# Attention scores in five PSUM banks taken in turn, two banks for the side work, and the second high half on ScalarE

## The chip, the core and the metric

The kernel runs on one core of one Trainium2 chip. The metric is the device time of one execution in microseconds. TensorE is called PE in the profile, VectorE DVE, ScalarE ACT, GpSimd POOL, and SP is the engine that issues most of the DMAs.

## What is computed

The input is x of 2 x 2048 rows with 256 features. A block of three parts is computed: half a feed-forward network, self-attention with 16 heads of 16 features, and half a feed-forward network again.

```
x = x + 0.5 * ffn(layernorm(x))
x = x + attention(layernorm(x))
x = x + 0.5 * ffn(layernorm(x))

ffn(h):  h = s0 * [h, -h] @ sign(k0);  h = 2 * relu(h)      # 256 -> 1024
         h = s1 * h @ sign(k1);        h = 2 * relu(h)      # 1024 -> 1024
         return s2 * h @ sign(k2)                           # 1024 -> 256
attention(h): q, k, v = h @ wq + bq, h @ wk + bk, h @ wv + bv   # per head
         softmax(q @ k.T / 4) @ v, heads side by side, @ wo.T + bo
```

The exponentials dominate ScalarE's work: 2 x 16 x 2048 x 2048 scores, 1,048,576 in each of the 128 partitions.

## The kernel before, in words

Tokens are worked in 8 blocks of 512. A unit u below 8 is the first network on block u, a unit from 8 to 15 is the second on block u - 8. A network has three layers, l1 (8 output tiles m of 128 x 512), l2 (8 tiles) and l3 (2 tiles); around them stand the layer norm (`norm`, `xn`, `split`, `flip`), the projections `qk` (4 tiles) and `v` (2 tiles), the sum of squares `sq` (2 per block, for a guard on the size of the scores) and, ahead of the second network, `heads` and `out`. Activations are kept as two float16 tensors, a high half (`h_hi`) and the rest (`h_lo`): whoever drains a PSUM bank writes first the high half, then `h_lo` as the bank less the high half.

PSUM has 8 banks of 512 float32 columns. Before attention begins, side work goes through seven of them in turn (`WHOLE`), ScalarE writes the high halves and VectorE the low ones.

Attention is 32 groups of 4 heads, 8 steps a group, 256 **steps** in all. The order of a step is written out in the loop `for n in range(att_steps)`; side work of the networks is dealt into it. On PE a step is:

- `score` 0: two pairs of score matmuls (p0, p1). A pair is two matmuls of 64 rows, side by side in the two row halves of the array, into two banks.
- the first part of the side work (S1), a number of matmuls that `PAIRS` gives by kind;
- `score` 1: the third pair (p2);
- the second part of the side work (S2);
- `score` 2: the fourth pair (p3);
- if there is one, a **column** (`sq` or `range`: one small tile in a bank of its own), taken from the list `columns` in steps in which a pair of side tiles has just been finished;
- `values`: 16 records of matmuls that multiply the probabilities of the step before with v, into the accumulating bank `O_BANK` (V).

Side tiles are worked two at a time (`lay_pair`, `pe_pair`): one matmul in the upper row half for the one, one in the lower for its mate, then turned. `PAIRS` deals the slots of a step as 5 and 3 for l2 (10 and 6 matmuls, a pair of tiles in four steps), 10 and 6 for l3, 4 and 4 for l1 (8 and 8 matmuls, a pair of tiles in every step), 1 and 1 for qk (4 and 4 matmuls of float32), 2 and 2 for v and out. Of the 256 steps 144 carry l2, 36 carry l3 and 76 the others. When the tiles of a pair change row halves, PE waits on its own semaphore `halves`; for l1, v and out that falls at the head of S2.

Scores use banks 0 to 3. Pair number e of all writes banks 2 * (e % 2) and the next (`pe_scores`, L737), and waits until exponential e - 2 has been done, since that one read the same banks. ScalarE does nothing in attention but the exponentials (`act_attention`, L808), one of 128 x 1024 for each pair, four a step. Side work, columns among it, goes through banks 5, 6, 7 in turn (`SHARED`); a pair of tiles starts when both of its banks have been drained (`pe_pair`, L683). In attention VectorE drains alone: high half (L857; L873 for qk), low half (L859; L875), high half, low half. The column `sq` is drained by one maximum (L880), behind the pair of its step. At a group's end VectorE copies bank 4 out (L994).

SP reads the same list of steps: it stages q and k of the next group, moves results of a group out, and loads x. None of its steps changes place here.

Of the kernel before, what the change touches and what calls it, by code (L numbers as in the profile page):

```python
# [17 lines left out]
P = 128  # L18
# [5 lines left out]
class Step:  # L24
# [4 lines left out]


    kind: str
    u: int = 0
# [10 lines left out]
    free_act: int = 0  # L43
    free_dve: int = 0
    mate: object = None

# [39 lines left out]
def build(nc, x, wq, bq, wk, bk, wv, bv, wo_t, bo, k0, k1, k2, s0, s1, s2, out):  # L86
# [24 lines left out]
    RING = 4  # L111
    PROB_SLOTS = 8
    GROUP = 4
    groups = batches * qblocks * heads // GROUP
    group_steps = key_tiles // 2
# [4 lines left out]

    WHOLE = [0, 1, 2, 3, 5, 6, 7]
    SHARED = [5, 6, 7]
    O_BANK = 4

# [83 lines left out]
    while not (side[0].kind == "l2" and side[0].u == qblocks + 1):  # L208
        lay(side.pop(0), WHOLE, True)
    scores_free = max(numbers.held[b][0] for b in range(4)), max(numbers.held[b][1] for b in range(4))  # L210

# [31 lines left out]
    def lay_pair(slots):  # L243

        s, t = side[0], side[1]
        if not s.n:
            for bank in (s, t):
                bank.on_act = False
                numbers.lay(bank, SHARED)
                find[bank.kind, bank.u, bank.m] = bank  # L250
            s.hi = 0
        lo, s.hi = s.hi, s.hi + slots
        work.append(replace(s, lo=lo, hi=s.hi, n=2 * s.n, mate=t))
        if s.hi == 2 * s.n:
            s.lo, s.hi = 0, s.n
            work.append(replace(t, lo=t.n, hi=t.n))
            del side[0:2]

    for n in range(att_steps):
        work.append(Step("att", n))  # L260
        work.append(Step("score", n, 0))
        lay_idle(n)
# [7 lines left out]
        if columns and not side[0].n:  # L270
            lay(columns.pop(0), SHARED, False)
        if n:
# [79 lines left out]
    with ExitStack() as ctx:  # L352
# [25 lines left out]
        h1_lo = sb("h1_lo", [P, kh, BANK], F16)  # L378
        prob = sb("prob", [P, PROB_SLOTS, 2, BANK], F32)
        q_st = sb("q_st", [P, 4, BANK], F16)  # L380
# [30 lines left out]

        raw_words = prob[:, :, :, :].rearrange("p s h c -> p (s h c)")
        n0, n1, n2 = 2 * kd * hidden // 4, kh * hidden // 4, kh * dim // 4
        assert n0 + n1 + n2 <= PROB_SLOTS * 2 * BANK
        k0_raw = raw_words[:, 0:n0].bitcast(U8).rearrange("p (k n) -> p k n", k=2 * kd)
# [165 lines left out]
        def pe_steps(steps):  # L581
            for s in steps:
                if s.kind == "att":
                    pe_attention(s.u)
                elif s.kind == "score":
                    for tile, pair in (((0, 0), (0, 1)), ((1, 0),), ((1, 1),))[s.m]:
                        pe_scores(s.u, tile, pair)
                elif s.kind == "values":
                    pe_values(s.u)
                elif s.kind == "att_end":  # L590

                    pe.wait_ge(exp_sem, 4 * att_steps)
                elif s.mate:
# [4 lines left out]
        def pe_fill(s):  # L598
            u, m, bank = s.u, s.m, s.bank
            if s.lo == 0:  # L600
                if s.free_act:
                    pe.wait_ge(act_done, s.free_act)
                if s.free_dve:
                    pe.wait_ge(dve_done, s.free_dve)
            for j in range(s.lo, s.hi):
                if s.kind == "turn_x":
# [129 lines left out]

        def pe_scores(n, tile, pair):  # L737
            g, tp = divmod(n, group_steps)
            t = 2 * tp + tile
            e = 4 * n + 2 * tile + pair  # L740
            if e >= 2:
                pe.wait_ge(exp_sem, e - 1)
            slot = g % 2 * 2 + pair
            for r in range(2):
                rows = slice(64 * r, 64 * r + 64)
                mm = pe.matmul(psum[:, 2 * pair + r, :], k_st[rows, slot, t * P:(t + 1) * P], q_st[rows, slot, :],  # L746
                               start=True, stop=True)
            mm.then_inc(qk_sem, 1)

        def pe_values(n):  # L750
            g, tp = divmod(n, group_steps)
            b, g4 = g // (qblocks * block_groups), g % block_groups
            for tile in range(2):
# [4 lines left out]
                for j in range(GROUP):  # L758
                    e = 4 * n + 2 * tile + j // 2
                    if j % 2 == 0:  # L760
                        pe.wait_ge(exp_sem, e + 1)
                    mm = pe.matmul(psum[32 * j:32 * j + va, O_BANK, :], v_sb[:, b * key_tiles + t, GROUP * g4 + j, :],  # L762
                                   prob[:, e % PROB_SLOTS, j % 2, :], start=(t == 0), stop=(t == key_tiles - 1))
                mm.then_inc(pv_sem, 1)
# [42 lines left out]

        def act_attention(n):  # L808
            for tile in range(2):
                for pair in range(2):  # L810
                    e = 4 * n + 2 * tile + pair
                    act.wait_ge(qk_sem, e + 1)
                    if e >= PROB_SLOTS:
                        act.wait_ge(pv_sem, (e - PROB_SLOTS) // 2 + 1)
                    act.activation(prob[:, e % PROB_SLOTS], psum[:, 2 * pair:2 * pair + 2, :], ACT.Exp,  # L815
                                   scale=score_scale / QK_SCALE ** 2).then_inc(exp_sem, 1)

# [323 lines left out]

        g_words = prob[:, :, :, :].rearrange("p s h c -> p (s h c)")
        gp = prob[:, 0:2].rearrange("p s h c -> p (s h) c")
        gq = g_words[0:va, 2 * 2 * BANK:2 * 2 * BANK + seq]
# [9 lines left out]
        def g_piece(m):  # L1154
            return prob[:, m // 2, m % 2, :]

# [181 lines left out]
```

## Time and profile before

| | |
|---|---|
| median of 3 runs | 1554.54 us (1554.02 to 1554.98) |
| the profiled execution | 1554.71 us |
| its span, first to last instruction | 1550.9 us |
| PE busy | 1527.7 us, 99% of the span |
| ACT busy | 1048.9 us, 68% |
| DVE busy | 639.6 us, 41% |
| attention, first and last step's start | 277.54 and 1463.16 us of the span |

The page's slices of the span show PE at nine tenths or more everywhere but in the first, and ACT at eight tenths during attention. The ends of matmuls are modelled in the profile, so a PE that reads as fully busy may still have stood: the starts of the rows tell more than the busy share. In a timeline row the first number is the start, the second the length of the merged stretch, then engine, line, operation, output and inputs, shapes, the number of instructions, and in brackets the idle time ahead with what ended it. Successive starts, subtracted, give how long a piece of a step took.

### The profile page before, as it was taken

Reading aid. Unit: us, or ns where it says so; the run is one execution under the profiler, and the core shown is the slowest. Engines: PE = TensorE matmul, PEld = TensorE weight load, DVE = VectorE, ACT = ScalarE, POOL = GpSimd, SP = SyncE. Lnnn points to the kernel's source line nnn. Section 1 sums busy time; section 2 is a strip of 40 time slices with the busy share of each in tenths; the row PEclk is TensorE's granted clock in tenths of the full one; section 3 lists DMA queues with packets and bytes.
Section 4 is the critical chain, followed back from the end, with each engine's and each line's share of the span. In section 5 each row is a group of like instructions: output and inputs, shape, how many; then the busy total and the mean of one; then the engine's idle time right before and its main releaser. Section 6 shows DMA issues by size and latency. Waiting matters only on the chain.

```text
span 1550.9 us, 29679 instructions
## 1 busy us (share of the span) xinstructions
PE 1527.7 (99%) x12441; PEld 580.4 (37%) x12441; DVE 639.6 (41%) x1410; ACT 1048.9 (68%) x1158; POOL 59.8 (4%) x65
## 2 busy tenths in 40 slices
PE   6999999999999999999999999999999999999999
PEld 3555455333323333333333333333233233233354
DVE  6556755512531263335333243342432433343372
ACT  3221221888788778878887888888888888788611
POOL 2010111000000000010010000000000000000000
PEclk9999999999999999999999999999999999999999
DMA  4221323312231331223212113112212211311110
GB/s 122 55 82 37 86 68 109 83 38 73 73 80 51 99 94 40 56 91 93 79 52 85 47 43 102 38 39 66 79 39 66 79 39 53 100 47 37 35 42 15
DMA packets 110505, 101.33 MB, mean 65 GB/s; under 512 B 56224, under 2 KB 95904, under 8 KB 110368
## 3 DMA queue, kind: packets, MB, share of 16 engines
q1 hardware_dynamic: 109392, 98.86, 22.3%
q8 instruction: 100, 1.64, 0.4%
q10 hardware_dynamic: 976, 0.53, 0.1%
q14 instruction: 37, 0.30, 0.1%
HBM read 61.87 MB, written 25.43 MB: 56 GB/s over the span
## 4 chain that ended last, share of the span: by engine, by line
PE 97%; DVE 1%; ACT 0%; issue 0%; POOL 0%; DMA 0%; SPq 0%; POOLq 0%; DVEq 0%
PE psum L762 30%; PE psum L731 29%; PE psum L746 17%; PE psum L634 12%; PE psum L646 3%; PE psum L622 3%; PE psum L653 2%; PE psum L667 1%; POOL square L1027 0%; ACT prob L815 0%; DMA x_sb<-in_x 0%; PE psum L660 0%; DVE xn L950 0%; PE psum L610 0%; DVE h_lo L859 0%
## 5 line engine op out<-in xcount | busy, mean ns | idle before, releaser
L815 ACT ACTIVATE prob<-psum 128x1024 f32<-128x1024 f32 x1024 | 965.9, 1030 | 223.4 <-PE psum L746 223.4
L762 PE MATMUL psum<-prob,v_sb 128*17 128x512 f32 x4096 | 490.5, 595 | 0.0
L746 PE MATMUL psum<-q_st,k_st 64*128 64x512 f16 x2048 | 352.3, 381 | 3.6 <-ACT prob L815 0.8
L857 DVE TENSOR_SCALAR h_hi<-psum 128x512 f16<-128x512 f32 x146 | 100.2, 686 | 413.7 <-PE psum L731 413.7
L746 PEld LDWEIGHTS psum<-q_st,k_st 64*128 64x128 f16 x2048 | 78.4, 93 | 380.5 <-ACT prob L815 342.8
L791 ACT ACTIVATE h_hi<-psum 128x512 f16<-128x512 f32 x110 | 65.1, 597 | 217.9 <-PE psum L634 167.9
L859 DVE SCALAR_TENSOR_TENSOR h_lo<-psum,h_hi 128x512 f16<-128x512 f32 x256 | 175.0, 690 | 83.9 <-ACT h_hi L791 78.9
L762 PEld LDWEIGHTS psum<-prob,v_sb 128*17 128x17 f32 x4096 | 96.3, 96 | 226.5 <-issue 200.8
L731 PE MATMUL psum<-h_hi,w 64*128 64x512 f16 x1184 | 151.8, 376 | 1.1 <-DVE h_lo L859 1.1
L731 PE MATMUL psum<-h_lo,w 64*128 64x512 f16 x1184 | 151.8, 376 | 0.0
L634 PE MATMUL psum<-h_hi,w 128*128 128x512 f16 x432 | 102.1, 379 | 0.0
L634 PE MATMUL psum<-h_lo,w 128*128 128x512 f16 x432 | 102.1, 379 | 0.0
L994 DVE COPY o_sb<-psum 128x512 f32<-128x512 f32 x32 | 22.1, 689 | 154.3 <-PE psum L762 154.3
L731 PEld LDWEIGHTS psum<-h_hi,w 64*128 64x128 f16 x1184 | 57.6, 94 | 63.4 <-ACT h_hi L791 1.5
L731 PEld LDWEIGHTS psum<-h_lo,w 64*128 64x128 f16 x1184 | 57.6, 94 | 61.5
L731 PE MATMUL psum<-xn,w 64*128 64x512 f16 x576 | 74.1, 376 | 0.9
L864 DVE SCALAR_TENSOR_TENSOR x_sb<-psum,scal,x_sb 128x512 f32<-128x512 f32 x32 | 23.2, 749 | 106.7 <-PE psum L731 75.9
L634 PEld LDWEIGHTS psum<-h_lo,w 128*128 128x128 f16 x432 | 42.3, 98 | 51.0
L634 PEld LDWEIGHTS psum<-h_hi,w 128*128 128x128 f16 x432 | 42.1, 98 | 51.1 <-issue 0.7
L1027 POOL TENSOR_TENSOR square<-piece 128x512 bf16<-128x512 f16 x32 | 32.9, 1039 | 732.5 <-DVE piece L873 413.9
L985 DVE RECIPROCAL den_t<-den_t 128x128 f32<-128x128 f32 x64 | 60.4, 944 | 0.0
L622 PE MATMUL psum<-xn,w 128*128 128x512 f16 x224 | 51.8, 387 | 0.2 <-ACT xn L787 0.2
(102 smaller groups left out, 870.0 us busy)
## 6 DMA issues: line engine op xcount, KB each, us to landing
k_st<-k_halves SPq DMA_DIRECT2D x64, 512.0 KB, 4.4
q_halves<-piece SPq DMA_DIRECT2D x32, 256.0 KB, 2.5
q_st<-q_halves SPq DMA_DIRECT2D x64, 128.0 KB, 4.9
x_rows<-x_sb SPq DMA_DIRECT2D x16, 256.0 KB, 2.2
k_halves<-piece SPq DMA_DIRECT2D x16, 256.0 KB, 2.6
att_rows<-o_sb SPq DMA_DIRECT2D x128, 32.0 KB
x_sb<-x_rows SPq DMA_DIRECT2D x8, 512.0 KB, 4.1
att_t<-att_rows SPq DMA_DIRECT2D x16, 256.0 KB
```

Source lines behind the costliest of these rows:

```text
L622: mm = pe.matmul(psum[:, bank, :], w0[:, k, m * P:(m + 1) * P], xt[:, half, k, :], start=(j == 0), stop=(j == s.n - 1))
L634: mm = pe.matmul(psum[:, bank, :], w1[:, k, m * P:(m + 1) * P], (h0_hi, h0_lo)[half][:, k, :], start=(j == 0), stop=(j == s.n - 1))
L646: mm = pe.matmul(psum[:, bank, t * dim:(t + 1) * dim], (h1_hi, h1_lo)[half][:, k, tile * P:(tile + 1) * P], w2[:, k, :], start=(jj == 0), ...
L731: mm = pe.matmul(to, w, a, start=(turned == 0 and j == 0), stop=(turned == 1 and j == length - 1))
L746: mm = pe.matmul(psum[:, 2 * pair + r, :], k_st[rows, slot, t * P:(t + 1) * P], q_st[rows, slot, :], start=True, stop=True)
L762: mm = pe.matmul(psum[32 * j:32 * j + va, O_BANK, :], v_sb[:, b * key_tiles + t, GROUP * g4 + j, :], prob[:, e % PROB_SLOTS, j % 2, :], st ...
L791: act.activation(hi, psum[:, bank, :], ACT.Relu).then_inc(act_done, 1)
L815: act.activation(prob[:, e % PROB_SLOTS], psum[:, 2 * pair:2 * pair + 2, :], ACT.Exp, scale=score_scale / QK_SCALE ** 2).then_inc(exp_sem, 1)
L857: dve.tensor_scalar(hi[:, m, :], psum[:, bank, :], 0.0, None, ALU.max).then_inc(dve_done, 1)
L859: dve.scalar_tensor_tensor(lo[:, m, :], psum[:, bank, :], 0.0, hi[:, m, :], ALU.max, ALU.subtract).then_inc(dve_done, 1)
L985: dve.reciprocal(den_t[:, half, cols], den_t[:, half, cols]).then_inc(den_inv, 1)
L1027: pool.tensor_tensor(square[:, m % 2, :], piece[:, m, 0, :], piece[:, m, 0, :], ALU.mult).then_inc(squared, 1)
```

## The change

It has three parts, all inside attention.

1. Scores take **five banks** (0 to 4) in turn, a bank at a time, not four in fixed pairs. `lay_scores` writes down for each bank of scores h (8 a step) its bank and who held it five places before (`bank_left`); `pe_scores` waits for that one, bank by bank. The exponentials of a step cover 1, 2, 2, 2, 1 banks; a two that would run from bank 4 to bank 0 is done as two ones. Over the 256 steps that makes 616 exponentials of two banks and 816 of one, for 1024 of two before. `O_BANK` moves from 4 to 5.
2. The side work has **two banks** (6, 7) in place of three; columns go into the ring of the scores (`lay_column`) and wait for the exponential that read the bank five places before (`free_exp`).
3. In a pair of l1, l2 or qk tiles **ScalarE writes the high half of the second tile** (81 tiles); VectorE writes the rest. ScalarE's exponentials are dealt to the three `score` steps for that, so that the high half stands between them.

`prob` keeps its 16 banks of probabilities under another shape. The network stages before and after attention keep seven banks.

```diff
     RING = 4
-    PROB_SLOTS = 8
+    PROBS = 16
     GROUP = 4
+    STEP_BANKS = 2 * GROUP
...
-    WHOLE = [0, 1, 2, 3, 5, 6, 7]
-    SHARED = [5, 6, 7]
-    O_BANK = 4
+    SCORES = [0, 1, 2, 3, 4]
+    O_BANK = 5
+    SHARED = [6, 7]
+    WHOLE = SCORES + SHARED
...
             for bank in (s, t):
-                bank.on_act = False
+                bank.on_act = bank is t and t.kind in ("l1", "l2", "qk")
                 numbers.lay(bank, SHARED)
...
+    taken = []
+    score_bank, bank_left, exp_groups, exp_done = [], [], [], []
+
+    def lay_scores(n):
+        for h in range(STEP_BANKS * n, STEP_BANKS * (n + 1)):
+            before = taken[-len(SCORES)] if len(taken) >= len(SCORES) else None
+            bank_left.append(before)
+            score_bank.append(SCORES[len(taken) % len(SCORES)])
+            taken.append(("exp", h))
+        for first, count in ((0, 1), (1, 2), (3, 2), (5, 2), (7, 1)):
+            h = STEP_BANKS * n + first
+            if count == 2 and score_bank[h + 1] != score_bank[h] + 1:
+                exp_groups.append((h, 1))
+                exp_groups.append((h + 1, 1))
+                exp_done.extend((len(exp_groups) - 1, len(exp_groups)))
+            else:
+                exp_groups.append((h, count))
+                exp_done.extend(count * (len(exp_groups),))
+
+    def lay_column(s):
+        kind, h = taken[-len(SCORES)]
+        assert kind == "exp"
+        s.free_exp = exp_done[h]
+        lay(s, SCORES[len(taken) % len(SCORES):][:1], False)
+        taken.append(("dve", s.dve))
...
         if columns and not side[0].n:
-            lay(columns.pop(0), SHARED, False)
+            lay_column(columns.pop(0))
...
-        def pe_scores(n, tile, pair):
+        def pe_scores(n, pair):
             g, tp = divmod(n, group_steps)
-            t = 2 * tp + tile
-            e = 4 * n + 2 * tile + pair
-            if e >= 2:
-                pe.wait_ge(exp_sem, e - 1)
-            slot = g % 2 * 2 + pair
+            t = 2 * tp + pair // 2
+            slot = g % 2 * 2 + pair % 2
+            h = STEP_BANKS * n + 2 * pair
+            for r in range(2):
+                if bank_left[h + r]:
+                    kind, left = bank_left[h + r]
+                    if kind == "exp":
+                        pe.wait_ge(exp_sem, exp_done[left])
+                    else:
+                        pe.wait_ge(dve_done, left)
...
-                if s.kind == "att":
-                    act_attention(s.u)
+                if s.kind == "score":
+                    act_exps(s.u, (0, 4, 6)[s.m], (4, 6, 8)[s.m])
...
+        def act_exps(n, lo, hi):
+
+            for h, count in exp_groups[exp_done[STEP_BANKS * n] - 1:exp_done[STEP_BANKS * (n + 1) - 1]]:
+                last = h + count - 1
+                if not lo <= last - STEP_BANKS * n < hi:
+                    continue
+                act.wait_ge(qk_sem, last // 2 + 1)
+                if last >= PROBS:
+                    act.wait_ge(pv_sem, (last - PROBS) // GROUP + 1)
+                bank, to = score_bank[h], h % PROBS
+                act.activation(prob[:, to:to + count, :], psum[:, bank:bank + count, :], ACT.Exp,
+                               scale=score_scale / QK_SCALE ** 2).then_inc(exp_sem, 1)
```

How the instructions stand. In the rows below the names in brackets are semaphores: `exp` counts exponentials, `mm_done` finished tiles of PE, `act_done` and `dve_done` drains by ScalarE and VectorE, `halves` PE's own turns, `qk` score pairs, `pv` finished halves of V.

ScalarE in two l1 steps of attention. Before, its whole stretch of attention is two rows:

```order
L815 ACTIVATE prob<-psum 128x1024 [waits qk] x8
L815 ACTIVATE prob<-psum 128x1024 [waits pv,qk] x1016
```

and now, around the high halves (L833) of two l1 tiles, of which such pieces follow each other:

```order
L833 ACTIVATE h_hi<-psum 128x512 [waits mm_done]
L860 ACTIVATE prob<-psum 128x512 [waits pv,qk] x3
L860 ACTIVATE prob<-psum 128x1024 [waits pv,qk] x3
L860 ACTIVATE prob<-psum 128x512 [waits pv,qk] x2
L860 ACTIVATE prob<-psum 128x1024 [waits pv,qk] x3
```

The exponentials are more and partly half as wide, and a high half stands in line among them, behind the exponential of the banks 3 and 4 of its step.

VectorE, the drains of two l1 pairs and their columns. Before:

```order
L857 TENSOR_SCALAR h_hi<-psum 128x512 [waits mm_done]
L859 SCALAR_TENSOR_TENSOR h_lo<-psum,h_hi 128x512 [waits dve_done]
L857 TENSOR_SCALAR h_hi<-psum 128x512 [waits mm_done]
L859 SCALAR_TENSOR_TENSOR h_lo<-psum,h_hi 128x512 [waits dve_done]
L880 TENSOR_REDUCE norms<-psum 64x1 [waits mm_done]
```

and now:

```order
L902 TENSOR_SCALAR h_hi<-psum 128x512 [waits mm_done]
L904 SCALAR_TENSOR_TENSOR h_lo<-psum,h_hi 128x512 [waits dve_done]
L904 SCALAR_TENSOR_TENSOR h_lo<-psum,h_hi 128x512 [waits act_done]
L925 TENSOR_REDUCE norms<-psum 64x1 [waits mm_done]
```

One of the four drains has gone, and the last low half waits for ScalarE.

PE, from the last pair of scores of a step with a column to the start of the next pair of l1 tiles. Before:

```order
L746 MATMUL psum<-q_st,k_st 128x512 [waits exp]
L746 MATMUL psum<-q_st,k_st 128x512
L660 MATMUL psum<-square,head_ones 32x512 [waits consts,squared,dve_done]
...
L731 MATMUL psum<-xn,w 128x512 [waits dve_done]
L731 MATMUL psum<-xn,w 128x512 x7
```

and now:

```order
L788 MATMUL psum<-q_st,k_st 128x512 [waits exp]
L788 MATMUL psum<-q_st,k_st 128x512
L697 MATMUL psum<-square,head_ones 32x512 [waits squared,exp,consts,dve_done,act_done]
...
L768 MATMUL psum<-xn,w 128x512 [waits dve_done,act_done]
L768 MATMUL psum<-xn,w 128x512 x7
```

No matmul has changed its place; the column waits for an exponential as well, and a pair of side tiles for both engines that drain. Where one instruction has more than one wait, those beyond the first are wait instructions of their own in PE's queue; there are about 1020 more of these than before, four a step.

## Rows read from the trace of the kernel before

**Rows 1.** The cores' view, then busy time by engine (page, part 1).
```profile
core 0: 1550.9 us, clock 1.000
...
PE 1527.7 (99%) x12441; PEld 580.4 (37%) x12441; DVE 639.6 (41%) x1410; ACT 1048.9 (68%) x1158; POOL 59.8 (4%) x65
```

**Rows 2.** Groups of instructions (page, part 5): the exponentials.
```profile
L815 ACT ACTIVATE prob<-psum 128x1024 f32<-128x1024 f32 x1024 | 965.9, 1030 | 223.4 <-PE psum L746 223.4
```

**Rows 3.** Timeline of PE, a step that carries l2.
```profile
902.54 0.61 PE L746 MATMUL psum<-q_st,k_st 64*128 64x512 f16 x4
902.98 1.24 PE L731 MATMUL psum<-h_hi,w 64*128 64x512 f16 x10
904.06 0.38 PE L746 MATMUL psum<-q_st,k_st 64*128 64x512 f16 x2
904.28 0.81 PE L731 MATMUL psum<-h_hi,w 64*128 64x512 f16 x6
904.97 0.39 PE L746 MATMUL psum<-q_st,k_st 64*128 64x512 f16 x2
905.29 1.91 PE L762 MATMUL psum<-prob,v_sb 128*17 128x512 f32 x16
907.13 0.61 PE L746 MATMUL psum<-q_st,k_st 64*128 64x512 f16 x4
```

**Rows 4.** Timeline of ScalarE, the same step.
```profile
902.97 3.77 ACT L815 ACTIVATE prob<-psum 128x1024 f32<-128x1024 f32 x4 [0.82 <-PE psum L746]
```

**Rows 5.** Timeline, a step that carries l1: PE and ScalarE.
```profile
702.47 0.60 PE L746 MATMUL psum<-q_st,k_st 64*128 64x512 f16 x4
...
702.90 3.78 ACT L815 ACTIVATE prob<-psum 128x1024 f32<-128x1024 f32 x4 [1.10 <-PE psum L746]
702.91 1.03 PE L731 MATMUL psum<-xn,w 64*128 64x512 f16 x8
...
703.98 0.39 PE L746 MATMUL psum<-q_st,k_st 64*128 64x512 f16 x2
...
704.20 1.03 PE L731 MATMUL psum<-xn,w 64*128 64x512 f16 x8
...
705.06 0.38 PE L746 MATMUL psum<-q_st,k_st 64*128 64x512 f16 x2
...
705.37 1.91 PE L762 MATMUL psum<-prob,v_sb 128*17 128x512 f32 x16
...
707.22 0.60 PE L746 MATMUL psum<-q_st,k_st 64*128 64x512 f16 x4
...
707.66 1.24 PE L731 MATMUL psum<-h_hi,w 64*128 64x512 f16 x10
```

**Rows 6.** Timeline of VectorE behind that step: the drains.
```profile
705.26 0.69 DVE L857 TENSOR_SCALAR h_hi<-psum 128x512 f16<-128x512 f32 x1 [2.01 <-PE psum L731]
705.99 0.69 DVE L859 SCALAR_TENSOR_TENSOR h_lo<-psum,h_hi 128x512 f16<-128x512 f32 x1
706.60 0.68 DVE L857 TENSOR_SCALAR h_hi<-psum 128x512 f16<-128x512 f32 x1
707.31 0.69 DVE L859 SCALAR_TENSOR_TENSOR h_lo<-psum,h_hi 128x512 f16<-128x512 f32 x1
```

**Rows 7.** Timeline of ScalarE in the first network: high halves without a wait between.
```profile
19.64 3.59 ACT L791 ACTIVATE h_hi<-psum 128x512 f16<-128x512 f32 x7
```

**Rows 8.** Timeline, the step behind a column's step.
```profile
403.11 0.60 PE L746 MATMUL psum<-q_st,k_st 64*128 64x512 f16 x4
...
403.62 0.67 DVE L880 TENSOR_REDUCE norms<-psum 64x1 f32<-64x512 f32 x1
403.85 1.04 PE L731 MATMUL psum<-xn,w 64*128 64x512 f16 x8
404.71 0.40 PE L746 MATMUL psum<-q_st,k_st 64*128 64x512 f16 x2
404.97 1.04 PE L731 MATMUL psum<-xn,w 64*128 64x512 f16 x8
```

More of the change, by code:

```diff
@@ L44 @@
     free_dve: int = 0
+    free_exp: int = 0
     mate: object = None
@@ L209, in build @@
         lay(side.pop(0), WHOLE, True)
-    scores_free = max(numbers.held[b][0] for b in range(4)), max(numbers.held[b][1] for b in range(4))
+    scores_free = max(numbers.held[b][0] for b in SCORES), max(numbers.held[b][1] for b in SCORES)
     PAIRS = {"l1": (4, 4), "l2": (5, 3), "l3": (10, 6), "qk": (1, 1), "v": (2, 2), "out": (2, 2)}
@@ L257, in lay_pair @@
             del side[0:2]
+    taken = []
[21 more added lines that the diff above has]
+        taken.append(("dve", s.dve))
     for n in range(att_steps):
         work.append(Step("att", n))
+        lay_scores(n)
         work.append(Step("score", n, 0))
@@ L378, in build @@
         h1_lo = sb("h1_lo", [P, kh, BANK], F16)
-        prob = sb("prob", [P, PROB_SLOTS, 2, BANK], F32)
+        prob = sb("prob", [P, PROBS, BANK], F32)
         q_st = sb("q_st", [P, 4, BANK], F16)
@@ L409, in build @@
         at_words = at[:].rearrange("p k t -> p (k t)").bitcast(U16).rearrange("p (k t w) -> p w k t", k=kd, w=2)
-        raw_words = prob[:, :, :, :].rearrange("p s h c -> p (s h c)")
+        raw_words = prob[:].rearrange("p s c -> p (s c)")
         n0, n1, n2 = 2 * kd * hidden // 4, kh * hidden // 4, kh * dim // 4
-        assert n0 + n1 + n2 <= PROB_SLOTS * 2 * BANK
+        assert n0 + n1 + n2 <= PROBS * BANK
         k0_raw = raw_words[:, 0:n0].bitcast(U8).rearrange("p (k n) -> p k n", k=2 * kd)
@@ L585, in pe_steps @@
                 elif s.kind == "score":
-                    for tile, pair in (((0, 0), (0, 1)), ((1, 0),), ((1, 1),))[s.m]:
-                        pe_scores(s.u, tile, pair)
+                    for pair in ((0, 1), (2,), (3,))[s.m]:
+                        pe_scores(s.u, pair)
                 elif s.kind == "values":
@@ L590, in pe_steps @@
                 elif s.kind == "att_end":
-                    pe.wait_ge(exp_sem, 4 * att_steps)
+                    pe.wait_ge(exp_sem, len(exp_groups))
                 elif s.mate:
@@ L604, in pe_fill @@
                     pe.wait_ge(dve_done, s.free_dve)
+                if s.free_exp:
+                    pe.wait_ge(exp_sem, s.free_exp)
             for j in range(s.lo, s.hi):
@@ L735, in pe_pair @@
                         mm.then_inc(halves, 1)
-        def pe_scores(n, tile, pair):
+        def pe_scores(n, pair):
             g, tp = divmod(n, group_steps)
-            t = 2 * tp + tile
-            e = 4 * n + 2 * tile + pair
-            if e >= 2:
-                pe.wait_ge(exp_sem, e - 1)
-            slot = g % 2 * 2 + pair
+            t = 2 * tp + pair // 2
[8 more added lines that the diff above has]
+                        pe.wait_ge(dve_done, left)
             for r in range(2):
                 rows = slice(64 * r, 64 * r + 64)
-                mm = pe.matmul(psum[:, 2 * pair + r, :], k_st[rows, slot, t * P:(t + 1) * P], q_st[rows, slot, :],
+                mm = pe.matmul(psum[:, score_bank[h + r], :], k_st[rows, slot, t * P:(t + 1) * P], q_st[rows, slot, :],
                                start=True, stop=True)
@@ L758, in pe_values @@
                 for j in range(GROUP):
-                    e = 4 * n + 2 * tile + j // 2
+                    h = STEP_BANKS * n + GROUP * tile + j
                     if j % 2 == 0:
-                        pe.wait_ge(exp_sem, e + 1)
+                        pe.wait_ge(exp_sem, exp_done[h + 1])
                     mm = pe.matmul(psum[32 * j:32 * j + va, O_BANK, :], v_sb[:, b * key_tiles + t, GROUP * g4 + j, :],
-                                   prob[:, e % PROB_SLOTS, j % 2, :], start=(t == 0), stop=(t == key_tiles - 1))
+                                   prob[:, h % PROBS, :], start=(t == 0), stop=(t == key_tiles - 1))
                 mm.then_inc(pv_sem, 1)
@@ L806, in act_steps @@
                     act.activation(g_piece(m), psum[:, bank, :], ACT.Identity, bias=bias).then_inc(act_done, 1)
[L808 to L816, printed above, removed]
+        def act_exps(n, lo, hi):
[9 more added lines that the diff above has]
+                               scale=score_scale / QK_SCALE ** 2).then_inc(exp_sem, 1)
         def dve_steps(steps):
@@ L1138, in sp_fetch @@
                 (hs, hd, BANK))).then_inc(att_in[half], 16)
-        g_words = prob[:, :, :, :].rearrange("p s h c -> p (s h c)")
-        gp = prob[:, 0:2].rearrange("p s h c -> p (s h) c")
+        g_words = prob[:].rearrange("p s c -> p (s c)")
+        gp = prob[:, 0:4]
         gq = g_words[0:va, 2 * 2 * BANK:2 * 2 * BANK + seq]
@@ L1154, in g_piece @@
         def g_piece(m):
-            return prob[:, m // 2, m % 2, :]
+            return prob[:, m, :]
         def sp_maxima():
```

## The prediction

> **What bounds the kernel now.** I read the cores' view first. The clock is granted at 1.000 over the whole span, its 2.4 GHz level [rows 1]. PE is busy for 1527.7 of 1550.9 us; ScalarE for 1048.9. That reads as if PE were the limit and nothing could be won by waiting less. But ends of matmuls are modelled, so I then read the starts in the timeline.
>
> A step that carries l2 [rows 3]: p0 and p1 take 0.44 us (902.54 to 902.98), S1 with 10 matmuls 1.08, p2 0.22, S2 with 6 matmuls 0.69, p3 up to V 0.32, V 1.84; together 4.59. Ten matmuls in 1.08 make six in 0.65, so 0.04 of S2 is standstill, and 0.01 of the 0.32. The step is all but full of matmuls.
>
> A step that carries l1 [rows 5]: 0.44, S1 with 8 matmuls 1.07 (702.91 to 703.98), p2 0.22, S2 with 8 matmuls 0.86, 0.31, V 1.85; together 4.75. S1 and S2 are the same work: 0.21 us of S1 is standstill. Its end says what it is: the first exponential starts at 702.90 and takes 1.03 [rows 2], so ends at 703.93; p2, which writes the banks that it read, starts 0.05 later, at 703.98. Then the reverse: from the fourth exponential's end to 707.65 ScalarE is idle, since p0 of the next step comes only behind V. Its idle time per step is 1.10 and 0.82 us [rows 4, 5], 223.4 us in all [rows 2]. PE waits for ScalarE in mid-step, ScalarE for PE at its ends: four banks let PE run only two pairs ahead.
>
> **The change part by part.** A step's start is time 0 below.
>
> *Exponentials.* An exponential of two banks in a row with others takes (3.78 - 1.03) / 3 = 0.92 us from start to start [rows 2, 5]. One of 512 columns is not in the trace. The nearest row is a high half of the same shape, 3.59 / 7 = 0.51 us [rows 7]. Bounds: 0.46, half of the 0.92, and 0.92, as if width cost nothing. I take 0.51, since it is the same size from the same memory. 616 twos and 816 ones over 256 steps are 2.4 and 3.2 a step: 2.21 + 1.63 = 3.84 us, against 3.68 before. With a high half at 0.51, which each l1 step has, 4.35.
>
> *Does a step then still wait?* ScalarE in an l1 step: bank 0 of the eight at 0.43 (as now: 702.47 to 702.90), banks 1 and 2 at 0.94, 3 and 4 at 1.86, the high half at 2.78, 5 and 6 at 3.29, bank 7 at 4.21, free at 4.72. In five banks p2 needs banks that the single exponential and the last one of the step before read: the single one ends at 0.43 + 0.60 = 1.03 (0.60: 3.59 less six times 0.50 [rows 7]), and p2 can come at 0.44 + 0.86 = 1.30. p3 needs the banks 1 and 2, free at 1.97, or 2.05 where they are split; it comes at 2.42. In the next step p0 needs the exponential from 1.86 and p1 the one from 3.29, done at 4.32, and p1 comes at 4.80. Every wait for an exponential goes, the closest by about a quarter of a microsecond. What is late next is nothing but PE's own work.
>
> *l2 steps:* 0.05 us each, 144 of them: 7.2 us. *l3 steps:* exponentials end where they do in l2, the matmuls are of another shape, I take 0.03 by 36: 1.1 us.
>
> *The other 76:* S1 falls to 0.86. But here the tiles change row halves at the head of S2, and that waits for S1's own matmuls. With S1 undelayed this shows: in a step in which PE came late for another reason, p2 to S2 takes 404.97 - 404.71 = 0.26 [rows 8], not 0.22. So such a step becomes 0.44 + 0.86 + 0.26 + 0.86 + 0.31 + 1.85 = 4.58: 0.17 less. Eight of the 76 stand behind a column and are without the exponential's wait already: 68 by 0.17 is 11.6 us.
>
> *Columns.* Behind one, the next pair of side tiles waits for a bank: p0 to S1 is 403.85 - 403.11 = 0.74 in place of 0.44 [rows 8], since the column's maximum, which frees that bank, started only at 403.62. Columns leave the side banks, so 8 by 0.30 is saved, 2.4 us. But a column now waits for the exponential of the banks 3 and 4, started at 1.86 and done at 2.89; the column could start at 2.42 + 0.21 = 2.63. With the 0.05 of a signal that is 0.3 us of standstill, at eight of nine columns (in the ninth that exponential is split): 2.4 us lost. The two cancel.
>
> *Two side banks.* A pair of tiles ends with S2; the next begins 707.66 - 705.06 = 2.60 us later [rows 5], whatever the exponentials do. Drains begin 0.20 after that end [rows 6] and take 0.73, 0.61, 0.71 and 0.69. With three banks the next pair needed the first two alone. Now it needs all of the pair's. VectorE's three are done at 0.20 + 0.73 + 0.61 + 0.69 = 2.23; ScalarE's high half, from 2.78 to 3.38 of the step, that is 0.96 behind the pair's end, is there before the last low half begins, at 1.54. Margin 0.3 us: cost nothing. The 2.60 us of score pairs and V cover it; without ScalarE's part the drain would be 2.94 and every pair would stand for 0.35.
>
> *Wait instructions on PE:* about 1020 more. Semaphore instructions are not in the rows. Below: nothing, since PE's queue runs ahead of the array, and p0 to S1 is 0.44 both in the l1 step, whose S1 waits for two side banks, and in the l2 step, which is in the middle of its tiles and waits for none [rows 3, 5]. Above: a weights load's length of 0.1 each, 100 us. I take nothing.
>
> *Sum:* 7.2 + 1.1 + 11.6 + 2.4 - 2.4 = 19.9 us, from the profiled execution's 1554.7: 1534.8. The median lies 0.2 under it: **1534.6 us**.
>
> The Trainium skill speaks against smaller exponentials: its page "ScalarE: Activation LUTs", section "What ACT_TABLE_LOAD costs", gives an ACTIVATE 186 ns plus 0.833 ns a column, of which some 93 ns overlap in a row, so each of the 408 extra ones costs its fixed part again. By it an l1 step holds 4.45 us of ScalarE's work, not 4.35; that is still under 4.58, so the sum would be the same and the margin 0.13.
>
> **The rivals.**
>
> *ScalarE becomes the bound where it has a high half.* For: at 0.60 for a single bank, a full unoverlapped length, an l1 step has 2.21 + 1.92 + 0.51 = 4.64 us for it, more in a step with a split, and then p2 waits again. Against: the 0.51 of [rows 7]. Price: the 76 short steps keep half of their wait and l2 keeps some, so about half of the 20 is won: 1544.
>
> *PE's wait instructions show (slower).* Place: ahead of p0 to p3, most of all between p0 and p1, which follow each other without cover. For: four more a step, every step. Against: p0 to S1 doesn't depend on them now. It decides from 19.9 / 1020 = 0.02 us each; at 0.05, half a weights load, it costs 51 us and the result is 1586.
>
> *The drain of two banks outlasts its cover (slower).* Place: S1 of the step behind each of the 81 pairs with a high half. For: the margin is 0.3 us, and ScalarE takes things in order. Against: the working above. If ScalarE's part brought no shortening, 0.35 by 81 is 28 us: 1563. It decides from a standstill of 0.25.
>
> *Five banks don't lift the wait*, since p2 still hangs on the step's first exponential: for it only the closeness, 1.03 against 1.30. Price: no change, 1554.
>
> **How the numbers follow.** Forecast 0.77, ScalarE's bound 0.08, PE's waits 0.04, the drain 0.07, no lift 0.04. The forecast's own range is 1531 (columns without the wait, l2 and qk a little better) to 1540 (a quarter of the gain lost where margins are small). The range that holds the time 8 times in 10 takes in the ScalarE case with something over: 1531 to 1547. About 0.2%, 3 us, is what a measurement can tell from no change. Faster: forecast, ScalarE and a part of the drain, 0.87; within it 0.04; slower 0.09.
>
> **What would show it.** Right: l2 steps at 4.54 and l1 steps at 4.58 from p0 to p0; S1 of l1 at 0.86 and p2 to S2 at 0.26; p0 to S1 at 0.44 everywhere; ScalarE's single exponentials 0.51 apart; 0.3 us of standstill ahead of eight columns. Wrong: p0 to p1 wider than now (wait instructions); p0 to S1 over 0.44 (drains); ScalarE without idle time in l1 steps.

## The result and the profile after

| | before | after |
|---|---|---|
| median | 1554.34 us (4 runs) | 1539.15 us (1537.64 to 1539.43, 4 runs) |
| the profiled execution | 1554.71 us | 1539.0 us |
| its span | 1550.9 us | 1535.1 us |
| ACT busy | 1048.9 us | 1130.6 us |
| DVE busy | 639.6 us | 585.1 us |

The ratio is 0.990, with a 95% interval of 0.9883 to 0.9917: faster by 15.2 us where 19.9 were forecast, and inside the range of 1531 to 1547. The direction, the steps that shrink and most of their sizes were right; the missing 4.3 us of the attention stage have four places, shown below.

The page and the cores' view of the changed kernel, against [rows 1]:

```profile
core 0: 1535.1 us, clock 1.000
...
PE 1512.7 (99%) x12441; PEld 599.4 (39%) x12441; DVE 585.1 (38%) x1329; ACT 1130.6 (74%) x1647; POOL 59.7 (4%) x65
```

PE's busy time fell by 15.0 us, with the same 12441 matmuls at the same clock: what left it was modelled length, that is standstill.

Groups of instructions, kept apart by shape, the exponentials; they answer to [rows 2]:

```profile
L860 ACT ACTIVATE prob<-psum 128x1024 f32<-128x1024 f32 x616 | 617.4, 1026 | 3.6 <-PE psum L788 2.0
L860 ACT ACTIVATE prob<-psum 128x512 f32<-128x512 f32 x816 | 466.1, 607 | 123.8 <-PE psum L788 119.4
```

ScalarE's idle time ahead of an exponential is 127.4 us, not 223.4, and nearly all of it lies ahead of single ones: that is the step's first, which waits for p0.

Timeline of PE, a step that carries l2, against [rows 3]:

```profile
889.58 0.60 PE L788 MATMUL psum<-q_st,k_st 64*128 64x512 f16 x4
890.02 1.24 PE L768 MATMUL psum<-h_lo,w 64*128 64x512 f16 x10
891.10 0.38 PE L788 MATMUL psum<-q_st,k_st 64*128 64x512 f16 x2
891.31 0.81 PE L768 MATMUL psum<-h_lo,w 64*128 64x512 f16 x6
891.96 0.38 PE L788 MATMUL psum<-q_st,k_st 64*128 64x512 f16 x2
892.27 1.91 PE L804 MATMUL psum<-prob,v_sb 128*17 128x512 f32 x16
894.11 0.61 PE L788 MATMUL psum<-q_st,k_st 64*128 64x512 f16 x4
```

S2 is 0.65 (891.31 to 891.96) and p3 to V 0.31: the step is 4.53 to 4.54 us. Timeline of a step that carries l1, with its drains, against [rows 5, 6]:

```profile
406.47 0.61 PE L788 MATMUL psum<-q_st,k_st 64*128 64x512 f16 x4
...
406.91 1.03 PE L768 MATMUL psum<-xn,w 64*128 64x512 f16 x8
407.78 0.38 PE L788 MATMUL psum<-q_st,k_st 64*128 64x512 f16 x2
408.03 1.04 PE L768 MATMUL psum<-xn,w 64*128 64x512 f16 x8
408.91 0.38 PE L788 MATMUL psum<-q_st,k_st 64*128 64x512 f16 x2
...
409.83 1.29 DVE L904 SCALAR_TENSOR_TENSOR h_lo<-psum,h_hi 128x512 f16<-128x512 f32 x2
411.06 0.60 PE L788 MATMUL psum<-q_st,k_st 64*128 64x512 f16 x4
...
411.50 0.81 PE L768 MATMUL psum<-xn,w 64*128 64x512 f16 x6
```

S1 is 0.87, p2 to S2 0.25, the step 4.59. VectorE's three drains (the last two are in the row at 409.83) end at 411.12, 2.21 us behind the pair's end at 408.91, and the next pair starts on time at 411.50.

Over all steps of attention, from the starts of PE's rows (mean of a kind, before and after):

| steps | before | after | sum |
|---|---|---|---|
| l2, 142 | 4.590 | 4.538 | -7.4 us |
| l3, 36 | 4.590 | 4.557 | -1.2 |
| l1 without a column, 29 | 4.770 | 4.636 | -3.9 |
| qk, 16 | 4.747 | 4.556 | -3.1 |
| v, 8, and out, 13 | 4.753, 4.769 | 4.733, 4.692 | -1.2 |
| with a column sq, 8 | 4.978 | 5.229 | +2.0 |
| with range, 1, and the first two | | | -0.9 |

The sum is -15.6 us (the rounded rows give 15.7); the span fell by 15.8. Counted so, with the one l2 step that has a column, the first two and the last, 146 steps carry l2 and 74 the others, where I had written 144 and 76.

### The profile page after: what moved, and what is told of

Its sections match the earlier page's. It is cut to its first block, busy times and chain, and to the rows that moved or that the text cites. A ratio compares the mean times of both kernels' runs of the same rounds, so it can differ in the third digit from the quotient of the medians.

```text
span 1535.1 us, 31520 instructions
## 1 busy us (share of the span) xinstructions
PE 1512.7 (99%) x12441; PEld 599.4 (39%) x12441; DVE 585.1 (38%) x1329; ACT 1130.6 (74%) x1647; POOL 59.7 (4%) x65
## 4 chain that ended last, share of the span: by engine, by line
PE 97%; DVE 1%; POOL 0%; DMA 0%; issue 0%; ACT 0%; SPq 0%; POOLq 0%; DVEq 0%
PE psum L804 31%; PE psum L768 29%; PE psum L788 16%; PE psum L671 12%; PE psum L683 3%; PE psum L659 3%; PE psum L690 2%; PE psum L704 1%; PE psum L697 0%; POOL square L1072 0%; DMA x_sb<-in_x 0%; DVE h_lo L904 0%; DVE xn L995 0%; DVE square L1052 0%; PE psum L647 0%
## 5 line engine op out<-in xcount | busy, mean ns | idle before, releaser
L860 ACT ACTIVATE prob<-psum 128x512 f32<-128x512 f32 (+1 forms) x1432 | 1018.3, 787 | 127.4 <-PE psum L788 121.4
L833 ACT ACTIVATE h_hi<-psum 128x512 f16<-128x512 f32 x183 | 109.8, 605 | 216.4 <-PE psum L671 161.1
L902 DVE TENSOR_SCALAR h_hi<-psum 128x512 f16<-128x512 f32 x73 | 50.5, 692 | 434.4 <-PE psum L768 434.4
L904 DVE SCALAR_TENSOR_TENSOR h_lo<-psum,h_hi 128x512 f16<-128x512 f32 x256 | 168.5, 687 | 81.1 <-ACT h_hi L833 78.7
L788 PEld LDWEIGHTS psum<-q_st,k_st 64*128 64x128 f16 x2048 | 82.1, 94 | 280.8 <-ACT prob L860 209.1
```

The costliest lines, as they stand in the source:

```text
L788: mm = pe.matmul(psum[:, score_bank[h + r], :], k_st[rows, slot, t * P:(t + 1) * P], q_st[rows, slot, :], start=True, stop=True)
L833: act.activation(hi, psum[:, bank, :], ACT.Relu).then_inc(act_done, 1)
L860: act.activation(prob[:, to:to + count, :], psum[:, bank:bank + count, :], ACT.Exp, scale=score_scale / QK_SCALE ** 2).then_inc(exp_sem, 1)
L902: dve.tensor_scalar(hi[:, m, :], psum[:, bank, :], 0.0, None, ALU.max).then_inc(dve_done, 1)
L904: dve.scalar_tensor_tensor(lo[:, m, :], psum[:, bank, :], 0.0, hi[:, m, :], ALU.max, ALU.subtract).then_inc(dve_done, 1)
```

## The experiments

Every run stands beside runs of the kernel before on the same chip (medians 1554.31 to 1554.82 us); ratios are to those.

**VectorE drains alone, with two side banks.**

```diff
-                bank.on_act = bank is t and t.kind in ("l1", "l2", "qk")
+                bank.on_act = False
```

> VectorE writes both high halves again, with two side banks and five score banks. Theory (two banks need the second high half on ScalarE): the drain of a pair then lasts about 2.94 us from the pair's end, its cover is 2.60, so p0 to S1 grows from 0.44 to about 0.8 behind the 81 pairs of l1, l2 and qk: +28 us, about 1567. Rival (the cover is enough either way, ScalarE's part only costs ScalarE time): no change from 1539, p0 to S1 stays 0.44.

Measured: 1577.34 us, ratio 1.0144 (1.0128 to 1.0161), 38 us slower than the change. Timeline, the last l1 step of a unit and the next:

```profile
418.20 0.38 PE L788 MATMUL psum<-q_st,k_st 64*128 64x512 f16 x2
...
420.36 0.61 PE L788 MATMUL psum<-q_st,k_st 64*128 64x512 f16 x4
420.45 0.69 DVE L904 SCALAR_TENSOR_TENSOR h_lo<-psum,h_hi 128x512 f16<-128x512 f32 x1
...
421.25 1.26 PE L768 MATMUL psum<-h_hi,w 64*128 64x512 f16 x10 [0.28 <-DVE h_lo L904]
```

p0 to S1 is 0.89 in place of 0.44. The four drains end at 421.14, 2.94 behind the pair's end as worked out, and PE starts 0.11 later. So a missed cover costs 0.45 to 0.49 a pair, not 0.35: what stands behind the wait, the signal and the weights load, shows too. By the same measure the change's own margin is 2.60 - 2.21 - 0.11, just under 0.3.

**Exponentials of two banks throughout, in five banks.**

```diff
-        for first, count in ((0, 1), (1, 2), (3, 2), (5, 2), (7, 1)):
+        for first, count in ((0, 2), (2, 2), (4, 2), (6, 2)):
```

> Five banks kept, but the exponentials of a step cover 2, 2, 2, 2 banks (split only where a two would run past the last bank). Theory (the leading exponential of one bank is what frees the third pair in time): S1 of l1, v and out steps goes back to about 1.07 in the four steps of five whose first exponential is a two, S2 of l2 back to 0.69 there: +12 and +6 us, about 1556. Rival (the fifth bank alone lifts the waits): 1539, S1 stays 0.86.

Measured: 1576.47 us, ratio 1.0138 (1.0121 to 1.0155): slower than the kernel before, twice the loss that the theory gave. Timelines of PE and of ScalarE, an l2 step:

```profile
890.73 1.24 PE L768 MATMUL psum<-h_lo,w 64*128 64x512 f16 x10
891.88 0.39 PE L788 MATMUL psum<-q_st,k_st 64*128 64x512 f16 x2
892.10 0.82 PE L768 MATMUL psum<-h_lo,w 64*128 64x512 f16 x6
892.80 0.39 PE L788 MATMUL psum<-q_st,k_st 64*128 64x512 f16 x2
```

```profile
890.72 3.83 ACT L860 ACTIVATE prob<-psum 128x1024 f32<-128x1024 f32 x5 [0.80 <-PE psum L788]
```

S1 is 1.15 (ten matmuls need 1.08), S2 0.70 (six need 0.65): p2 and p3 both wait, in l2 steps as in the others. The fifth bank wins nothing by itself. With five banks and pairs of matmuls, a two at an even place frees one bank of each of two later pairs, so every pair hangs on two exponentials; the sequence 1, 2, 2, 2, 1 gives p0 the two banks of one exponential and p1 those of the next.

Why it is slower than the kernel before, I had not foreseen. There, p2 comes 0.05 behind the end of the exponential that it waits for (703.93 to 703.98, [rows 5]); here the exponential ends at 890.72 + 1.03 = 891.75 and p2 comes at 891.88. Read instruction by instruction, it is 0.06 in all 210 late waits of p2 and p3 before, and 0.14 in nearly all of this run. The difference goes with the wait instruction: before, a pair had one wait, carried by its weights load; now it has two, the first is an instruction of its own, and when that one comes true late the weights load follows it 0.08 us later. By estimate 256 steps by 0.08 are 20 us; without them the run would stand near the theory's 1556. No run changes the waits alone while they are late, so this reading rests on the rows.

**The reverse: single exponentials in four banks, with three side banks.**

```diff
-    SCORES = [0, 1, 2, 3, 4]
-    O_BANK = 5
-    SHARED = [6, 7]
+    SCORES = [0, 1, 2, 3]
+    O_BANK = 4
+    SHARED = [5, 6, 7]
...
-        for first, count in ((0, 1), (1, 2), (3, 2), (5, 2), (7, 1)):
+        for first, count in tuple((j, 1) for j in range(STEP_BANKS)):
```

(and `on_act` and the columns as before the change)

> Four score banks and three side banks as before the change, VectorE drains all side tiles, columns in side banks; only the exponentials differ from before: each of one bank, eight a step. Theory (narrower exponentials alone don't do, the third pair then hangs on the second single one): S1 of l1 at about 1.15, waits at p2 and p3, ScalarE with 8 x 0.51 = 4.1 us a step: no gain over before, 1554 to 1570. Rival (the width of the exponential that is waited for is all, the bank count doesn't matter): 1539.

Measured: 1604.43 us, ratio 1.0323 (1.0306 to 1.0341). Timelines of PE and of ScalarE:

```profile
704.73 1.03 PE L768 MATMUL psum<-xn,w 64*128 64x512 f16 x8
705.95 0.39 PE L788 MATMUL psum<-q_st,k_st 64*128 64x512 f16 x2 [0.19 <-ACT prob L860]
```

```profile
704.72 4.03 ACT L860 ACTIVATE prob<-psum 128x512 f32<-128x512 f32 x8 [0.88 <-PE psum L788]
```

S1 is 1.22. The second single exponential starts 0.49 behind the first, (4.03 - 0.60) / 7, and ends at about 705.83; p2, which needs it, comes at 705.95. The loss is far over the 1554 to 1570 expected. Here too a pair has two waits and comes 0.14 behind its exponential (0.12 by the rows above), not 0.06; that makes up 0.08 a step, by estimate 20 of the 50 us. The rest is that the fourth single exponential, for which p3 waits, ends later than the second of two banks did: in an l2 step p3 comes 2.64 us behind p0, before it was 2.43. Without the 0.08, S1 of l1 would be 1.14, still over the 1.07 of before. So neither the bank nor the width alone gives anything: it takes a fifth bank *and* a single exponential at the head.

**Single exponentials in five banks.**

```diff
-        for first, count in ((0, 1), (1, 2), (3, 2), (5, 2), (7, 1)):
+        for first, count in tuple((j, 1) for j in range(STEP_BANKS)):
```

> Five banks as in the change, but every exponential of one bank, eight a step: 616 more instructions of ScalarE. ScalarE's work per step is 8 x 0.51 = 4.07 us, 4.58 with a high half, against 4.54 and 4.59 of PE. Theory (the change leaves ScalarE a margin of a quarter of a microsecond): l2 steps stay at 4.54, l1 steps wait a little, 1539 to 1543. Rival (ScalarE was already at its bound after the change, and the missing 4.6 us of the forecast are that): over 1550.

Measured: 1537.03 us (1535.61 to 1537.58), ratio 0.989 (0.9874 to 0.9907): 2.1 us under the change, where up to 4 over it were expected at worst. l2 steps take 4.537, the same. ScalarE is not the bound after the change, and 616 more exponentials don't make it one; their start-to-start time was 0.49, against the 0.51 that I took. The gain lies at columns: their steps are 4.86 (l1) in place of 5.25, since the bank that a column takes is free some 0.4 us earlier; in the profiled executions that is 3.0 us at the eight columns, of which the steps of qk, v and out take 1.1 back. The wait behind range, told below, was shorter by 0.4 there as well.

**Both high halves on ScalarE.**

```diff
-                bank.on_act = bank is t and t.kind in ("l1", "l2", "qk")
+                bank.on_act = t.kind in ("l1", "l2", "qk")
```

> ScalarE writes both high halves of l1, l2 and qk pairs. It has 4.35 + 0.51 = 4.86 us in an l1 step, over PE's 4.59, and a late exponential of the banks 5 and 6. Theory: l1 steps grow to about 4.86, l2's last steps hardly: +0.27 for 36 and a little for qk, 1549 to 1553. Rival (VectorE's drain was the tighter of the two, so that halving it helps): under 1539.

Measured: 1559.25 us, ratio 1.0032 (1.0019 to 1.0044), 20 us over the change and 6 over the upper end of what was expected. Timeline:

```profile
412.19 0.38 PE L788 MATMUL psum<-q_st,k_st 64*128 64x512 f16 x2
...
412.54 1.12 ACT L833 ACTIVATE h_hi<-psum 128x512 f16<-128x512 f32 x2
413.20 1.29 DVE L904 SCALAR_TENSOR_TENSOR h_lo<-psum,h_hi 128x512 f16<-128x512 f32 x2 [3.27 <-ACT h_hi L833]
413.49 2.98 ACT L860 ACTIVATE prob<-psum 128x1024 f32<-128x1024 f32 x4
414.34 0.77 PE L788 MATMUL psum<-q_st,k_st 64*128 64x512 f16 x4
414.95 1.04 PE L768 MATMUL psum<-xn,w 64*128 64x512 f16 x8
```

Here the exponential of the banks 5 and 6 starts at 413.49, 1.30 behind the pair's end, and p1 waits for it: p0 to S1 is 0.61. VectorE, with two drains left, still ends 2.30 behind the pair's end (413.20 + 1.29), no earlier than in the change, since its first has to wait for ScalarE. The theory had the place wrong in part: l1 steps are 4.73 on the mean, not 4.86, and the l2 steps, expected to lose hardly anything, give 7.6 of the 19.2 us, all of it in steps behind a finished pair, where p0 to S1 is 0.52 to 0.88. Part of the size is again the wait instruction: p1 comes 0.14 behind its exponential in 71 steps, which at 0.08 each is some 6 us. What else lengthens the worst of these steps wasn't followed. Of the three ways to share the drains that were run, one and one is the one that fits.

**More wait instructions on PE.**

```diff
             h = STEP_BANKS * n + 2 * pair
+            if h >= 2 * PROBS:
+                for old in (2, 3, 4):
+                    pe.wait_ge(exp_sem, max(1, exp_done[max(0, h - old * PROBS)]))
```

> Three more waits ahead of each score pair, all long fulfilled: 1039 more wait instructions on PE (2777 in place of 1738), nothing else. Theory (PE's queue takes them ahead of the array): p0 to p3 keep their lengths, 1539 within 1 us. Rival (wait instructions show on PE): 0.05 us each, +52 us, 1591; from 0.02 us each they would have eaten the whole gain.

Measured: 1538.42 us, ratio 0.9899 (0.9882 to 0.9915). Timeline of PE, an l2 step:

```profile
889.50 0.60 PE L791 MATMUL psum<-q_st,k_st 64*128 64x512 f16 x4
889.94 1.24 PE L768 MATMUL psum<-h_lo,w 64*128 64x512 f16 x10
891.02 0.38 PE L791 MATMUL psum<-q_st,k_st 64*128 64x512 f16 x2
```

The starts are 0.44 and 1.08 apart, as without them. A fulfilled wait on PE costs nothing that these runs can show. That the same instruction costs 0.08 us when its wait comes true late, as in the run with exponentials of two banks, this run could not show, since all of its added waits were fulfilled.

**Columns behind the values, range's bank given back early.**

```diff
-        taken.append(("dve", s.dve))
+        taken.append(("dve", s.dve - 4 * (s.kind == "range")))
...
-        if columns and not side[0].n:
-            lay_column(columns.pop(0))
         if n:
             work.append(Step("values", n - 1))
             if n % group_steps == 0:
                 work.append(Step("o", n // group_steps - 1))
+        if columns and not side[0].n:
+            lay_column(columns.pop(0))
```

> Columns are laid behind the values in their step, and the bank of the column range is given back after VectorE's first copy rather than after its last instruction. Theory: the standstill ahead of eight columns (about 0.43 us each beyond the 0.2 that a column's own matmuls take) and the 1.44 us wait of the score pair that got range's bank both go: -3.4 and -1.4 us, about 1534.3. Rival (the column's wait comes from its own chain of semaphores or from GpSimd's squares, not from the exponential of banks 3 and 4): the 1.44 goes alone, 1537.6.

Measured: 1535.42 us (1534.71 to 1535.97), ratio 0.9874 (0.9858 to 0.989). Timeline of PE, a column's step (L697):

```profile
399.53 0.38 PE L788 MATMUL psum<-q_st,k_st 64*128 64x512 f16 x2
...
401.57 0.38 PE L697 MATMUL psum<-square,head_ones 128*32 128x512 bf16 x2
401.89 0.60 PE L788 MATMUL psum<-q_st,k_st 64*128 64x512 f16 x4
```

From p3 to the next p0 it is 2.36 us, in the changed kernel 2.85 (below): the standstill is gone, in all eight. Such a step takes 4.80, not 5.25. The rival was not all wrong, though: what the exponential released late was a chain of wait instructions, as shown in the next section.

**The columns' place alone**, with range's bank kept until VectorE's last instruction; the diff is the second part of the one above.

> Only the columns are laid behind the values; range keeps its bank until VectorE's last instruction. Theory (the 1.44 us standstill at range was a slow tiny instruction of VectorE, whose length differs from run to run, and not the bank's late return): as the run with both edits, 1535.4, within 1 us. Rival (the bank's return was half of that gain): 1536.8.

Measured: 1535.57 us (1534.94 to 1536.8), ratio 0.9881 (0.9864 to 0.9897). The medians are 0.15 apart, as the theory had it. But the profiled execution shows the score pair behind range waiting once more, so this is not the clean case that I made of it. Timeline of PE, a row of this run:

```profile
953.06 0.39 PE L788 MATMUL psum<-q_st,k_st 64*128 64x512 f16 x2 [0.93 <-DVE flag L1059]
```

With the bank given back early no such wait was in the three profiles taken so, though L1052, the slow instruction of VectorE, took 1.29 to 1.49 us in them and 1.33 here: in the trace it takes both, the slow instruction and the bank's late return. What it is worth in the median can't be told from these runs.

**Combinations, and the change again**, all three on one chip. The first has single exponentials and both edits to the columns:

> Five banks, every exponential of one bank, columns behind the values and range's bank given back early. Both edits remove the column's standstill, so they don't add up; what single exponentials still bring is 0.35 us at the first step of attention, and they cost a little where ScalarE has its longer high half of qk. Theory: 1534.5 to 1536, no different from the columns' edit alone. Rival (the two gains of 2.1 and 3.7 us are of different places): 1533.

Measured: 1536.11 us (1535.28 to 1536.62), ratio 0.9884 (0.9867 to 0.99). The gains don't add up, since both lay at the columns. The second keeps the change's exponentials but for the one of banks 3 and 4:

```diff
-        for first, count in ((0, 1), (1, 2), (3, 2), (5, 2), (7, 1)):
+        for first, count in ((0, 1), (1, 2), (3, 1), (4, 1), (5, 2), (7, 1)):
```

> As the change, with columns behind the values, range's bank given back early, and the exponential of the banks 3 and 4 of each step done as two ones (1, 2, 1, 1, 2, 1). Theory: 1534.5 to 1535.5, since nothing of PE waits for that exponential any more once the columns are moved, but in the first step. Rival (its lateness still costs somewhere): under 1533.

Measured: 1534.53 us (1534.33 to 1534.83), ratio 0.9872 (0.9856 to 0.9889). It is the fastest of all, by 0.9 us over the columns' edits without it, which is less than these runs can tell.

The change as it is:

> The change as it is, once more, beside the two others on one chip: 1538 to 1539.5, and about 0.25% over the best of them. Its trace shows whether the 1.44 us standstill behind range comes again (theory: its length is that of one tiny instruction of VectorE, which was 0.21 to 2.03 us so far) or stays as it was (rival).

Measured: 1538.76 us (1538.29 to 1539.95), ratio 0.9899 (0.9882 to 0.9915). The best is 4.2 us under it, a little over 0.25%. The wait behind range came again: PE stood idle for 0.95 us ahead of p2 in this profile, with L1052 at 1.72.

## Why the prediction was right, and where its terms were off

*What bounds the kernel:* right. The starts, not the busy share, told it: PE reads 99% busy in both kernels, and yet standstill at p2 and p3, 0.05 us in an l2 step and 0.21 in an l1 step, was part of that share and is gone.

*Exponentials and ScalarE's room:* right. The single ones come 0.49 apart (0.51 taken) and last 0.607. The Trainium skill, "ScalarE: Activation LUTs", section "What ACT_TABLE_LOAD costs", gives 186 ns plus 0.833 ns a column, with some 93 ns of overlap in a row; that is, as an estimate, 0.613 for the length and 0.520 from start to start. The length agrees, the spacing came out shorter. The rival in which ScalarE becomes the bound doesn't appear.

*Drains of qk:* a small cost that I had put at nothing, in the step behind each finished qk pair (8 steps). Timeline of the changed kernel:

```profile
376.80 0.74 DVE L920 SCALAR_TENSOR_TENSOR piece<-psum,bk_sb,piece 128x512 f16<-128x512 f32 x1
...
377.66 0.18 PEld L768 LDWEIGHTS psum<-at,wq_sb 64*128 64x128 f32 x1 [0.29 <-DVE piece L920]
...
378.63 0.41 PE L788 MATMUL psum<-q_st,k_st 64*128 64x512 f16 x2
```

VectorE's drains last 0.75 here, not 0.69; the last ends at 377.54, 2.45 behind the pair's end at 375.09, and the weights load of the next pair, in float32, comes 0.12 later, too late to be covered by p1. In the step after, such a load comes at 382.11, ahead of S1 at 382.33. The pair itself starts in time (p0 to S1 0.45), but its second matmuls come 0.07 late, and p2 with them: S1 is 0.93 there, not 0.86. With what follows at V that is 0.8 us in all, the smallest of the four shortfalls.

*l2 and l3 steps:* right to the hundredth: 0.052 and 0.033 saved, against 0.05 and 0.03.

*The other 76:* the 0.17 holds for l1 (4.752 to 4.587) and is exceeded for qk (4.746 to 4.527 in the undisturbed steps, which have no turn at S2). **It was mis-sized for v and out**: I took one price for the turn of the row halves, from float16 tiles, where theirs are float32. Timeline of the changed kernel, v:

```profile
392.49 0.38 PE L788 MATMUL psum<-q_st,k_st 64*128 64x512 f16 x2
...
392.75 0.73 PEld L768 LDWEIGHTS psum<-wv_sb,at 64*128 64x128 f32 x8 [0.30 <-PE psum L768]
392.75 1.13 PE L768 MATMUL psum<-wv_sb,at 64*128 64x256 f32 x8
...
393.72 0.38 PE L788 MATMUL psum<-q_st,k_st 64*128 64x512 f16 x2
```

S1 fell to 0.86 (391.63 to 392.49) as said. But S2 is 0.97 (392.75 to 393.72), with the same matmuls: the weights of the first turned tile are loaded only once `halves` has come, and in these 22 steps that load is not covered. It is 0.11 a step, 2.4 us in all. Before the change the wait for the exponential hid it. No run moved the turn; that the uncovered float32 load is the cause rests on these rows, on the length of such a load (0.19, against 0.09 in float16) and on the l1 steps, where S2 grows by 0.01 alone. The kernel before already had one such step, which I overlooked, an out step behind a column's step; its S2 was 0.97 too:

```profile
792.83 1.14 PE L731 MATMUL psum<-wo_sb,att_t 64*128 64x256 f32 x8
793.80 0.38 PE L746 MATMUL psum<-q_st,k_st 64*128 64x512 f16 x2
```


*Columns:* the direction was right, the size short. Each was to stand 0.3 us and stood 0.46 in l1 and l2 steps. Timeline:

```profile
398.31 0.38 PE L788 MATMUL psum<-q_st,k_st 64*128 64x512 f16 x2
...
398.98 0.22 PEld L697 LDWEIGHTS psum<-square,head_ones 128*32 128x32 bf16 x2 [0.79 <-issue]
399.01 0.50 PE L697 MATMUL psum<-square,head_ones 128*32 128x512 bf16 x2 [0.32 <-issue]
...
401.16 0.61 PE L788 MATMUL psum<-q_st,k_st 64*128 64x512 f16 x4
```

p3 to the column is 0.70, where it was 0.31 in the kernel before (I had taken 0.21). The exponential ends when it was said to, 0.43 to 0.49 behind p3 in most of them. But the column starts 0.10 to 0.21 behind that end, not 0.05, since the wait for it is followed by other wait instructions of the column; and V starts 0.13 to 0.34 behind the column, not 0.01 to 0.02, since the weights of both, which otherwise load beside matmuls, follow the wait one after the other. 8 steps: 3.5 us where 2.4 were taken, 1.1 short. The experiments that move them win 3.6 to 3.7 us.

*A wait that I missed:* `lay_column` keeps range's bank until the last of VectorE's five instructions. The p2 of the next step needs that bank. Timelines of VectorE and PE:

```profile
953.81 2.02 DVE L1052 TENSOR_TENSOR square<-square 1x64 f32<-1x64 f32 x1
...
956.29 0.14 DVE L1059 TENSOR_SCALAR flag<-flag_f 1x1 int32<-1x1 f32 x1
956.49 0.39 PE L788 MATMUL psum<-q_st,k_st 64*128 64x512 f16 x2 [1.26 <-DVE flag L1059]
```

It cost 1.4 us in this profile, and nothing in the two in which that instruction (L1052) took 0.21.

*Two side banks:* right, and shown from both sides: without ScalarE's part 38 us are lost, with both high halves there 20.

*The drain rival's price* was 28 us for a drain of the old length; the run that made it real lost 38 us against the change, as a missed cover costs more than the lateness alone.

*PE's wait instructions:* nothing, as taken, where the waits are fulfilled in time, and in the change those of p0 to p3 are, but at the very start of attention and in the step behind range. The reason given covers no more than that: late ones cost 0.08 us each in three of the experiments, and showed at the columns. So the change's small margins guard more than the prediction counted.

*Sum:* the shortfalls of 2.4, 1.1, 1.4 and 0.8 are 5.7 us. My count of the steps (144 and 76 for 146 and 74) had made the forecast 0.2 too large, and another 0.2 lie in hundredths of l1 and in the last step, which the starts don't span. Against them stand 0.6 us more than forecast at the first two steps of attention, 0.8 in qk (16 steps by 0.05) and 0.4 in hundredths of l2 and l3. That leaves 4.3, the difference of 19.9 and 15.6. That the shortfall stayed small is in part luck: errors of both signs met, and the wait behind range differs from run to run.

## What to carry to other kernels

Where two engines hand banks to each other in turn, write down for each bank who held it last, and choose the sizes so that a pair of writers waits for one reader; more buffers with the wrong sizes won nothing here, and by the rows it is the second wait that each pair then needs that made the kernel slower than with fewer. A wait instruction is free only as long as its wait comes true ahead of time. A wait that is removed uncovers what had hidden behind it (here the turn's weights load), so cost the shortened step by a step that already ran without the wait, once for each data type. And the place of a small odd job matters: eight columns of 0.2 us each cost some 3.5 us more because of where in the step they stood.

## What was not expected of the hardware

The same VectorE instruction on 64 elements of one partition (L1052, L1007 in the kernel before) took between 0.21 and 2.03 us in thirteen profiled executions: 0.21 in two, 0.52 in one, 0.98 in two, of which one is of the kernel before, and 1.29 to 2.03 in eight. A tiny one behind it, L1059, took 0.14. Nothing here tells why. A thousand fulfilled wait instructions on PE cost nothing, while a late wait costs more than its lateness: the score matmuls start 0.06 us behind the end of the exponential where the weights load carries the wait, 0.14 where an instruction ahead of it does, the columns 0.10 to 0.21, and a missed cover of the drains 0.11 to 0.15 a pair over the 0.34 of its lateness.
